# Routing of finished pairs inside the steps of the first attention, and the context's low part on GpSimd

## What is computed

```python
x = x + tanh(g_xattn[0]) * cross_attention(layernorm(x), ctx, mask)      # 16 heads of 16
xn = layernorm(x).reshape(1600, 256)
scores = sigmoid(xn @ W_gate_router)                                       # 8 experts
_, sel = top_k(scores + expert_bias, 2)
w = take(scores, sel); w = w / (w.sum(-1) + 1e-20)
out = silu(xn @ Wg_s) * (xn @ Wu_s) @ Wd_s                                 # shared
out[token] += w * (silu(xn @ Wg[e]) * (xn @ Wu[e]) @ Wd[e])                # for its two experts e
x = x + tanh(g_ffn[0]) * out
x = x + tanh(g_xattn[1]) * cross_attention_2(layernorm(x), ctx)
x = x + tanh(g_ffn[1]) * lora_ffn(layernorm(x))
```

## Time and profile before

| | us |
|---|---|
| runs of the kernel before, median of 3 | 925.54 (921.02 to 927.78) |
| time of the profiled execution | 926.79 |
| its span, first to last instruction | 925.0 |
| TensorE busy (matmuls) | 795.2, 86% |
| VectorE busy | 588.6, 64% |
| ScalarE busy | 477.8, 52% |
| GpSimd busy | 228.5, 25% |
| mean granted clock of TensorE | 0.93 of full |

### The profile page before, as it was taken

One profiled execution on the slowest core, in us unless ns is written; L12 is line 12 of the kernel. 1 busy time (PEld: TensorE's weight loads), 2 busy tenths in 40 slices (PEclk: granted clock), 3 DMA queues, 4 the chain that ended last, 5 costly groups with the idle time before them and its releaser, 6 DMA issues.

```text
span 925.0 us, 23409 instructions
## 1 busy us (share of the span) xinstructions
PE 795.2 (86%) x8046; PEld 625.0 (68%) x8046; DVE 588.6 (64%) x1713; ACT 477.8 (52%) x1017; POOL 228.5 (25%) x209
## 2 busy tenths in 40 slices
PE   5479999999999879658995679999999998878996
PEld 3246776777777647548993557667677676557996
DVE  4877777777777558536453478788788776563332
ACT  3336565665665566214662246566566564534543
POOL 2535222221222234730003543324211111000000
PEclk9789999999999999759998679999999997779998
DMA  6977888797889411232336976987877884000001
GB/s 190 227 181 140 164 161 163 155 171 162 158 165 188 90 33 33 83 94 90 121 110 187 196 149 137 193 169 157 188 157 158 168 157 92 1 1 1 19 18 36
DMA packets 150630, 117.02 MB, mean 127 GB/s; under 512 B 80956, under 2 KB 142120, under 8 KB 150536
## 3 DMA queue, kind: packets, MB, share of 16 engines
q1 hardware_dynamic: 143472, 105.71, 54.0%
q0 software_dynamic: 4096, 6.57, 2.8%
q10 hardware_dynamic: 2976, 3.61, 1.4%
HBM read 77.84 MB, written 37.76 MB: 125 GB/s over the span
## 4 chain that ended last, share of the span: by engine, by line
PE 46%; DMA 21%; SPq 10%; DVE 8%; issue 7%; ACT 4%; another core or an unknown queue 3%; POOL 0%; ACTq 0%; DVEq 0%; POOLq 0%
PE ps L1759 18%; DMA cT<-in_ctxT 9%; PE ps L1844 7%; PE ps L1870 4%; DMA QS<-mp 4%; DMA scr_q<-qp 4%; PE ps L1893 3%; DMA QS<-scr_q 3%; PE ps L1903 2%; SPq L391 2%; SPq L377 2%; SPq L410 1%; DVE mx L1436 1%; PE ps L1820 1%
## 5 line engine op out<-in xcount | busy, mean ns | idle before, releaser
L920 ACT ACTIVATE prob<-ps 128x400 f32<-128x400 f32 (+1 forms) x384 | 184.2, 500 | 94.4 <-PE ps L1893 83.4
L1870 PE MATMUL ps<-KS,QS 96*100 96x361 bf16 x512 | 167.3, 342 | 22.3 <-DVE mx L1432 9.6
L1432 DVE CUSTOM_DVE_ANT_0 ps<-ps,biasq 100x361 f32<-100x361 f32 x256 | 135.1, 544 | 56.8 <-PE ps L1870 51.9
L1436 DVE TENSOR_REDUCE mx<-ps 100x1 f32<-100x361 f32 x256 | 127.5, 528 | 50.7 <-PE ps L1870 45.3
L1893 PEld LDWEIGHTS ps<-QS,KS 98*128 98x128 bf16 x1536 | 110.3, 101 | 50.3 <-issue 10.7
L1893 PE MATMUL ps<-QS,KS 98*128 98x100 bf16 x1536 | 135.3, 212 | 7.0 <-ACT prob L920 3.6
L1844 PE MATMUL ps<-cT,wk 128*128 128x361 f32 x256 | 103.0, 514 | 23.4 <-DMA cT<-in_ctxT 10.3
L1870 PEld LDWEIGHTS ps<-KS,QS 96*100 96x100 bf16 x512 | 64.5, 128 | 58.3 <-DVE mx L1436 15.3
L671 POOL TENSOR_TENSOR kp<-kr,kp 128x722 bf16<-128x722 f32 x32 | 48.5, 1516 | 141.9 <-ACT kp L891 141.8
L1903 PE MATMUL ps<-prob,V 128*17 128x100 f32 (+1 forms) x3072 | 82.5, 257 | 0.9 <-ACT xT L830 0.9
L1844 PEld LDWEIGHTS ps<-cT,wk 128*128 128x128 f32 x256 | 48.4, 206 | 46.6 <-issue 18.5
(11 more groups left out here) (217 smaller groups left out, 1699.2 us busy)
## 6 DMA issues: line engine op xcount, KB each, us to landing
scr_k<-kp SPq DMA_DIRECT2D x96, 180.5 KB, 5.4
KS<-scr_k SPq DMA_DIRECT2D x64, 270.8 KB, 3.7
cT<-in_ctxT SPq DMA_DIRECT2D x32, 361.0 KB
KS<-scr_k SPq DMA_DIRECT2D x64, 180.5 KB, 4.0
QS<-scr_q SPq DMA_DIRECT2D x64, 150.0 KB, 4.2
KS<-scr_k SPq DMA_DIRECT2D x64, 90.2 KB, 4.2
scr_q<-qp SPq DMA_DIRECT2D x24, 200.0 KB, 3.8
scr_q<-qp SPq DMA_DIRECT2D x48, 100.0 KB, 6.2
```

Of the source, the lines that this page charges most:

```text
L920: nc.scalar.activation(prob[0:KROWS[t], t, hg, :], ps[0:KROWS[t], c % 2, 0:HQ * S], ACT.Exp).then_inc(a["exp"], 1)
L1432: nc.vector.tensor_tensor_reduce(ps[0:S, banks[h % len(banks)], 0:S2], ps[0:S, banks[h % len(banks)], 0:S2], biasq[p][:, :], 1.0, -3.0e38, ...
L1436: nc.vector.reduce_max(mx[:, h:h + 1], ps[0:S, banks[h % len(banks)], 0:S2], axis=AX.X).then_inc(a["max"], 1)
L1870: mm(ps[0:S, banks[h % len(banks)], 0:S2], QS[p][0:SROWS, h, :], KS[p][0:SROWS, h * S2:(h + 1) * S2], start=True, stop=True).then_inc(a["s ...
```

## The change

- The norm, transposes, logits, scores, counts and positions of pairs of batches 0 to 5 move into the steps 3 to 15 of the first attention; pairs 6 and 7 follow in the tail and between shared items 0 to 6. An odd step b has on VectorE `place_pair((b - 5) // 2)` and `norm_pair((b - 3) // 2)` between maxima 6 and 7, and `positions` at its end; on TensorE `count_pair` and the pair's transposes into bank 6, with a wait for ScalarE's copy of them ahead of `weigh`. An even step has `stats_end` and `route((b - 4) // 2)` at VectorE's end, and on TensorE `logits_pair` into bank 6, with a wait for ScalarE's score.
- The logits come out by rows (tokens on partitions, the tokens as weight and the router as moving operand), so that their turn and copies go. Inside the steps the sigmoid is exp(-x) on ScalarE and + 1 and reciprocal on VectorE.
- The count is a running one: two products a pair, with the totals `before` kept on VectorE. `count_all` multiplies eight columns.
- Scatters of pair j run on GpSimd from step 2j + 6 on (n = 2j + 8, two steps behind its positions begin), those of pairs 5 to 7 between weight pieces. Each queues behind GpSimd's key part and ahead of the context's low part.
- `ctx_low` of batches 2 to 15 moves from VectorE to GpSimd in both attentions.
- Ten weight pieces instead of six on GpSimd; VectorE's four come at items 8 to 11.
- The router's weights load with the small vectors at the start. The loops of the first attention are written out on all engines.
- `shares` runs once over all batches.

```diff
-        NPIECES, NPOOL = 2 + E + E // 2, 6
+        NPIECES, NFIRST, NPOOL = 2 + E + E // 2, 6, 10
+
+        def normalized(b):
+            return xn4[:, b, :] if b < B - GB else xn[:, b - (B - GB), :]
...
+        NSTEPPED = NPAIR - 2
+
+        def routed(j):
+            return 13 * j + 2 * min(j, NSTEPPED)
+
+        def route_base(j):
+            return routed(j) + (2 if j < NSTEPPED else 0)
...
-                    with sp.Fori(0, B // 2 - 2) as i:
-                        for u in range(2):
-                            step(l, 2 * i + u, u, i + l * IB, True, True, i)
-                else:
-                    for n in range(B - 4):
-                        step(l, n, n % 2, n // 2 + IB, True, True)
+                for n in range(B - 4):
+                    step(l, n, n % 2, n // 2 + l * IB, True, True, n // 2)
...
+                        ctx_low(l, n + 2, n % 2)
+                        if n % 2 == 1 and n <= 11:
                             split_pair((n + 3) // 2)
                         k3(l, n + 3)
                         if n % 2 == 1 and n <= 9:
-                            norm_pair((n + 5) // 2)
+                            norm_pair(Q1, (n + 5) // 2)
+                    ctx_low(l, B - 1, 1)
...
-                    with pool.Fori(0, B // 2 - 2) as i:
-                        for u in range(2):
-                            n = 2 * i + u + 2
-                            bias(n, u, i + 1, False)
-                            biasT_(n, u, False)
-                            k3(l, n + 1)
-                    for n in range(B - 2, B):
+                    for n in range(2, B):
+                        if n % 2 == 0 and n >= 8:
+                            scatter(n // 2 - 4)
+                        ctx_low(l, n, n % 2)
                         bias(n, n % 2, n // 2, False)
                         biasT_(n, n % 2, False)
                         if n + 1 < B:
                             k3(l, n + 1)
-                for g in range(GE):
-                    norm(2 * l + 1, g)
-                if l == 0:
-                    for j in range(NPOOL):
-                        pool.wait_ge(s0["whi"], START + j + 1)
-                        hi, raw, lo = piece(j)
-                        nc.gpsimd.tensor_tensor(lo, raw, hi.bitcast(F32), ALU.subtract).then_inc(s0["plo"], 1)
+                        if n % 2 == 0 and n >= 4:
+                            norm_pair(F0, n // 2 - 2)
+                    scatter(NSTEPPED - 2)
+                    norm_pair(F0, NSTEPPED)
+                if l == 1:
+                    for g in range(GE):
+                        norm(F1N, g)
+
+            def low_piece(j):
+                pool.wait_ge(s0["whi"], START + j + 1)
+                hi, raw, lo = piece(j)
+                nc.gpsimd.tensor_tensor(lo, raw, hi.bitcast(F32), ALU.subtract).then_inc(s0["plo"], 1)
...
+            def scatter(j):
+                pool.wait_ge(s0["rt"], START + routed(j + 1))
+                pool.wait_ge(sn["xn"], START + B * F0 + 2 * j + 2)
+                for b in (2 * j, 2 * j + 1):
+                    for c in range(2):
+                        nc.gpsimd.indirect_dma_start(scr_x, bass.IndirectOffsetOnAxis(posi[:, c, b:b + 1], 0),
+                                                     normalized(b), None).then_inc(s_scat, 16)
...
             attn(0)
-            pool.wait_ge(sa[0]["x"], START + B)
-            norm(F0, GE)
...
-            for part in range(2):
-                pool.wait_ge(s0["rt"], START + NRT * part + 11)
-                for b in range(PARTS[part][0] * GB, PARTS[part][1] * GB):
-                    scatter(b)
+            low_piece(0)
+            low_piece(1)
+            scatter(NSTEPPED - 1)
+            low_piece(2)
+            low_piece(3)
+            norm_pair(F0, NPAIR - 1)
+            low_piece(4)
+            low_piece(5)
+            scatter(NPAIR - 2)
+            low_piece(6)
+            low_piece(7)
+            scatter(NPAIR - 1)
+            for j in range(8, NPOOL):
+                low_piece(j)
             attn(1)
...
+            def score_pair(j):
+
+                act.wait_ge(s0["lg"], START + j + 1)
+                logits = ps[0:S, 6, 0:2 * E]
+                if j < NSTEPPED:
+                    nc.scalar.activation(sc[:, 2 * j:2 * j + 2, :], logits, ACT.Exp, scale=-1.0).then_inc(s0["sc"], 1)
+                else:
+                    nc.scalar.activation(sc[:, 2 * j:2 * j + 2, :], logits, ACT.Sigmoid).then_inc(s0["sc"], 1)
...
+                    norm_pair(Q1, (b + 4) // 2)
+                if l == 0 and u == 1 and b >= 3:
+                    norm_pair(F0, (b - 3) // 2)
+                if l == 0 and u == 0 and b >= 4:
+                    score_pair((b - 4) // 2)
...
-            def route(part):
+            def route(j):

                 r = s0["rt"]
-                b0, b1 = (g * GB for g in PARTS[part])
-                bs, sh, base = slice(b0, b1), [S, b1 - b0, E], NRT * part
-                dve.wait_ge(s0["sc"], START + part + 1)
+                b0, b1 = 2 * j, 2 * j + 2
+                bs, sh, base = slice(b0, b1), [S, 2, E], route_base(j)
+                dve.wait_ge(s0["sc"], START + j + 1)
+                if j < NSTEPPED:
+                    nc.vector.tensor_scalar(sc[:, bs, :], sc[:, bs, :], 1.0, None, ALU.add).then_inc(r, 1)
+                    dve.wait_ge(r, START + base - 1)
+                    nc.vector.reciprocal(sc[:, bs, :], sc[:, bs, :]).then_inc(r, 1)
+                    dve.wait_ge(r, START + base)
                 nc.vector.tensor_tensor(bsc[:, bs, :], sc[:, bs, :], bc(ebias[:, :].unsqueeze(1), sh), ALU.add).then_inc(r, 1)
                 pick(r, 2, base, b0, b1)
                 dve.wait_ge(r, START + base + 6)
                 nc.vector.tensor_tensor(wsel[:, bs, :], oh[:, 0, bs, :], oh[:, 1, bs, :], ALU.add).then_inc(r, 1)
-
-            def positions(part):
+                dve.wait_ge(r, START + base + 7)
+                if j == 0:
+                    nc.vector.memset(before[:, 0, :], 0.0).then_inc(r, 1)
+                else:
+                    nc.vector.tensor_tensor(before[:, 0, :], before[:, 1, :], wsel[:, b0 - 1, :], ALU.add).then_inc(r, 1)
+                dve.wait_ge(r, START + base + 8)
+                nc.vector.tensor_tensor(before[:, 1, :], before[:, 0, :], wsel[:, b0, :], ALU.add).then_inc(r, 1)
+
+            def place_pair(j):
+
+                b0, b1 = 2 * j, 2 * j + 2
+                dve.wait_ge(s0["cnt"], START + j + 1)
+                nc.vector.tensor_tensor(place[:, b0:b1, :], ps[0:S, 6, COUNTS].rearrange("s (b e) -> s b e", e=E),
+                                        bc(regions[:, :].unsqueeze(1), [S, 2, E]), ALU.add).then_inc(s0["rt"], 1)
+
+            def positions(j):

                 r = s0["rt"]
-                b0, b1 = (g * GB for g in PARTS[part])
-                bs, sh, base = slice(b0, b1), [S, b1 - b0, E], NRT * part
-                dve.wait_ge(s0["cnt"], START + 2 * part + 1)
-                nc.vector.tensor_tensor(place[:, bs, :], ps[0:S, 7 - part, 0:(b1 - b0) * E].rearrange("s (b e) -> s b e", e=E),
-                                        bc(regions[:, :].unsqueeze(1), sh), ALU.add).then_inc(r, 1)
-                dve.wait_ge(r, START + base + 8)
+                bs, base = slice(2 * j, 2 * j + 2), route_base(j)
+                dve.wait_ge(r, START + base + 10)
                 nc.vector.tensor_tensor(bsc[:, bs, :], oh[:, 0, bs, :], place[:, bs, :], ALU.mult)
                 nc.vector.tensor_tensor(mx8[:, bs, :], oh[:, 1, bs, :], place[:, bs, :], ALU.mult).then_inc(r, 1)
-                dve.wait_ge(r, START + base + 9)
-                nc.vector.reduce_sum(pf[:, 0, bs], bsc[:, bs, :], axis=AX.X)
-                nc.vector.reduce_sum(pf[:, 1, bs], mx8[:, bs, :], axis=AX.X).then_inc(r, 1)
-                dve.wait_ge(r, START + base + 10)
-                nc.vector.tensor_copy(posi[:, :, bs], pf[:, :, bs]).then_inc(r, 1)
-
-            def shares(part):
+                dve.wait_ge(r, START + base + 11)
+                nc.vector.reduce_sum(sj[:, 0, bs], bsc[:, bs, :], axis=AX.X)
+                nc.vector.reduce_sum(sj[:, 1, bs], mx8[:, bs, :], axis=AX.X).then_inc(r, 1)
+                dve.wait_ge(r, START + base + 12)
+                nc.vector.tensor_copy(posi[:, :, bs], sj[:, :, bs]).then_inc(r, 1)
...
+                if l == 0 and u == 1 and b >= 5:
+                    place_pair((b - 5) // 2)
+                if l == 0 and u == 1 and b >= 3:
+                    norm_pair(F0, (b - 3) // 2)
...
-                if has_2:
-                    ctx_low(l, b + 2, u)
...
                     stats(2 * l + 1, b - 1, sa[l]["x"], b)
+                if l == 0 and u == 0 and b >= 2:
+                    stats_end(F0, b - 2, b)
+                if l == 0 and u == 0 and b >= 4:
+                    route((b - 4) // 2)
+                if l == 0 and u == 1 and b >= 5:
+                    positions((b - 5) // 2)
...
-                    if n == AT_NORM - 1:
```

(82 more changed lines are left out.)

298 lines of the change are left out of this document (139 added, 159 removed).

## The result

The changed kernel takes 941.65 us (median of four, 931.29 to 944.99), the kernel before beside it 926.66. The ratio is 1.0117, interval 1.0066 to 1.0169: slower by 1.2%. Forecast were 908 and a range of 893 to 929. The experiments came in five groups of runs on four chips; each ratio is against the kernel before in the same group, and the chip of this first group isn't on record. Ratios leave out executions more than 1.5% above the fastest of the same kernel; the profiled one of e5 (924.8) is such a one. The profiled execution took 941.2, its span is 939.4.

A forecast was written before the change was run, and what follows sets the result against it. TensorE was taken to bound the first attention's steps (busy 16.43 of 16.65 us), with a 22.5 us freeze in the shared items. Terms: 15 - 6 - 25 - 1.3 = -17.3, giving 908 us, range 893 to 929.

The forecast's parts named there:

- the sum for steps 3 to 14: First attention: moved work and added waits, less idle time and air, net +15 us, ends +4 and +24.
- Moved work: TensorE in the first attention's steps: transposes, logits and running count cost 1.7 us a pair, 10.1 for pairs 0 to 5.
- The wait for `xn` in odd steps: First attention, odd steps: TensorE waits behind score 7 for VectorE's `place` and `xn` rows, 0.7 x 6 = 4 us.
- `route`: VectorE's end of even steps: makes the next maximum 1.1 to 2.4 us late, 1.7 taken, 8.5 over five routes.
- the freeze: Shared items of the kernel before: waits on unknown releasers while GpSimd issues 32 scatters back to back, priced at 22.5 us.
- Air of 7 us: First attention: idle TensorE of about 2.5 us and air of about 4.5 in three late steps, set against added costs.
- Rival (d): First attention: the freeze follows the scatters into it, 24 scatters cost 31 us, total 939; chance 0.08.
- Rival (b): VectorE and GpSimd lock each other out, weight pieces too: attention +24, items 4 more, total 921; chance 0.18.
- Last step and tail: End of the first attention: 7.8 us of TensorE work gone, pair 6 adds 1.7; -6 us, between -3 and -8.
- Shared items: The 16 shared items of the first feed-forward part: 47.3 us against 72.8, -25; ends -28 and -15.
- (c): Rival: the freeze stays where scatters remain behind the attention, +10, total 918; chance 0.14.
- Shares: Computed in one piece: about half of TensorE's 2.43 us wait for that VectorE stretch stays, -1.3 us.

The follow-up runs named there:

- e5: e2 with the routing's last three operations moved behind three maxima of the next step, scatters still in bursts; ratio 0.9957 to the kernel before.
- p3: The kernel before, unchanged, run again for its profile; items 70.4 to 71.6 us over its three repeats, no ratio of its own given.
- e7: e5 with each pair's scatters spaced over two steps instead of in bursts; ratio 0.9703 to the kernel before, ten steps 172.1 us.
- e2: The changed kernel with the first half of the routing moved into VectorE's gap between the two second key parts; ratio 0.9773 to the kernel before.
- e1: The changed kernel with all 32 scatters placed behind the first attention, routing still in the steps; ratio 1.0067 to the kernel before.
- e11: The same kernel as e7, run on the chip of e5; ratio 0.9805 to the kernel before.
- e10: The same kernel as e5, run on another chip; ratio 0.9735 to the kernel before.
- e3: The changed kernel with a pair's four scatters spaced one at a time over two steps; ratio 0.9981 to the kernel before, ten steps 196.4 us.
- e13: e7 with the scatters of pairs 4 and 5 also spread between GpSimd's weight pieces; ratio 0.9728 to the kernel before.
- e12: The kernel before with four of GpSimd's weight pieces put between its first 24 scatters, one behind every six; ratio 0.9989 to the kernel before.
- e4: The changed kernel with the context's low part back on VectorE in both attentions; ratio 0.9923 to the kernel before.
- p5: The kernel before, unchanged, run again for its profile on the chip of e13; items 70.4 to 71.6 us over its three repeats, no ratio given.
- e8: e5 with all 32 scatters placed behind the first attention; ratio 0.9711 to the kernel before.
- e6: The kernel before with seven unused reductions (3.7 us) added at VectorE's end of seven even steps of the first attention; ratio 1.0173.

## Why the prediction was wrong

**The failed step is the sum for steps 3 to 14**, +15 forecast, +45 measured. It held no term for the clock and none for late signals, and took the middle of a wait that came whole. Its terms:

- *Moved work*, 10.1 us for six pairs, 8.5 for the five in the ten steps: measured 5.9 against the first profile of the kernel before, whose steps have 3.4 us at half clock in them, and 7.5 against p3 (160.2 busy), which has none there: about right.
- *The wait for `xn` in odd steps*, 4 us: none. In e7 all idle time of ten steps is 4.4 us, less than before (7.2).
- *`route`*, 1.7 late in each, 8.5: measured 2.4, five times, 12.1. I had put the collision with GpSimd's third key part at its place and its size at 2.4 as the upper end, then took the middle. The trace decides for the whole collision: 1.42 us for an operation that takes 0.18 clear of it (e2, L1317). By the rule of the Trainium skill ("SBUF — State Buffer", section "Who interferes with whom") each `route` pays in full, and here the trace agrees.
- *The clock*, not in the sum at all: 18.7 us in the ten steps. I had used the half clock only behind the freeze of the items. A stall added to an engine that was busy 16.43 of 16.65 has a second price there. e1 shows it with nothing but the routing's stall (13.6); e2, with stalls of 1.0, has none.
- *Late signals*, not in the sum either: 11.4 us of idle pieces beside the scatters.
- *Air of 7 us* taken off: idle time didn't shrink, it grew from 7.2 to 27.3.

**Rival (d)**, the freeze following the scatters into the attention, had 0.08 and 939. That the time came out there is luck in part, since it holds only a part of the cause: where the hold-up is, bursts cost 1.5% (e5 against e11) to 2.2% (e5 against e10, 25 us in the profiles, where the rival said 31), elsewhere next to nothing (e10 against e7: 0.9735 and 0.9703). My argument against it was that the first fifteen scatters froze nothing; in the steps rows of four are enough (step 10 above). The steps have more transfer traffic than the items; whether that is why isn't shown. **Rival (b)**, the lock-out, had the stall right and lacked its clock. I treated (b) and (d) as exclusive, and both came. The routing's stall with its clock is 24 us of the ten steps (e3 against e7, 196.4 and 172.1), the hold-up with its clock 20 to 25 (e5 against e11 without its step 14, and e5 against e10). The changed kernel has both, 213.6 against 172.1 (215.6 and 210.9 in its other profiles), so they overlap by a few us; these are estimates across chips.

**Last step and tail**: -6 forecast, -2.5 measured; the burst of pair 5 stands in it (371.6 to 376.6), TensorE's issue waits 0.4, 0.4 and 1.1 us beside and behind it, and its clock is 0.87. Without the hold-up it is -7.1 in e7 (19.7), -3.8 in e13 (23.0); the kernel before itself took 26.8 to 29.8.

**Shared items**: -25 forecast, -22.6 measured, so the size was right. Its reason was mostly wrong. I had put 22.5 us on the freeze, "what it costs" as a remainder. By the rows of e12 it was worth 6 to 7; without it TensorE would have waited for rows instead. The bound behind it was the queue I had read as a bystander: 32 scatters on GpSimd at 1.3 us or more, from 357.5 to 402.9, and rows are loaded behind the last. The change gains because 24 of them leave before the items start. The 1.5 us for collisions of weight pieces with VectorE came as two, here of 3.5 and 1.7 us extra:

```profile
416.33 3.87 DVE L1702 TENSOR_TENSOR xTl<-xT,xTh 128x200 fp32r<-128x200 f32 x1
...
416.37 3.60 POOL L807 TENSOR_TENSOR Wgul<-Wgu,Wguh 128x768 fp32r<-128x768 f32 x2
```

A sum of the rivals was off too: (b) and (c) together are 908 + 13 + 10 = 931, where the range ends at 929.

**Right** were, as far as the runs show, the low part at nothing (251.3 and 250.9 us for the second attention; by e4 it is 2 us or less in the ten steps, with 5 us in the total not sorted out), the spans of the fills (the first row load at 420.9, ahead of the last items) and that unrolling costs nothing (steps 1 to 4 took 16.1 to 17.2 us, before 16.8 to 17.1). *Shares*: the slot stage is 5.0 us shorter instead of 1.3; TensorE was busy 95.7 instead of 101.0 at clock 0.93 instead of 0.89, so most of it is clock. Over all profiles the stage took 121.7 to 124.6 us before and 119.6 to 122.8 after, about 2 us less; it is not sorted out further.

## What to carry to other kernels

Where an engine is at 98% of a step, price a wait that you add twice: its length, and the half clock that can follow it (here 3.4 to 10.2 us of it behind most stalls of 2.4 us, and behind some of 1 us); then look for the gap in the late engine's own program (here 1.4 us between two waits) and put the work there, with its two-input operations clear of GpSimd's long subtractions. Issue indirect scatters one at a time between other work of GpSimd. And where signals look frozen, don't take the remainder for the price: ask first which queue would have set the end without it, and when an experiment takes the freeze away, what else it moved.

## What the runs showed of the hardware

- With indirect scatters back to back on GpSimd (0.99 us each, some of the first up to 2.04, 0.30 apart) signals of TensorE to ScalarE and VectorE came late: up to 2.8 us beside a burst of four in the changed kernel (scores done at 257.7, taken at 260.56), and in the row of 32 of the kernel before ScalarE took at 393.90 what TensorE had finished at 382.8, and waited up to 24.4 us in one piece (p5). VectorE ran the positions and the table from 387.56 to 392.5 meanwhile. On two chips bursts of four did nothing of the sort (e2, e4, e10), nor did rows of 8 and 12 behind the attention (e1, e8), and on the chip with the hold-up rows of six and one of eight there did not either (e12). What differs, between the chips or in the traffic beside the scatters, isn't known.
- TensorE's granted clock fell to 1.2 GHz at stalls of 2.4 us for 3.4 to 10.2 us, or not at all (the stalls at 155 and 192 us of the changed kernel, two of six in e6), with the engine busy through the stretch but for further stalls. Behind the stalls of 1.0 us in e2 it never fell. But length alone doesn't decide: every kernel has stalls of 0.33 and 0.99 us at the end of step 13, and the clock fell there for 3.4 us in the kernel before (the rows below), p5, the changed kernel, e1 and e3, and in e2, e4, e5, e7 and e10 it did not. In e5 it fell for 6.8 us behind three pieces of 0.37 to 0.46 us (176.3). So the same kernel's executions differ: the changed one took 931 us at a mean clock of 0.928 and 941 to 945 at 0.920 to 0.922 in its first group.

```profile
297.11 0.35 PE L1879 MATMUL ps<-ident,mxs 100*32 100x100 f32 x1 [0.99 <-DVE mxs L1446]
...
297.20:299.70 2.50, 2.50 (x46) 2.15 (x50) 1.82 (x14) 1.13 (x3) 1.30 (x3) 0.50 1.18 248
```
